# One block for the front and the heads of an mLSTM layer: context turned once and kept, gate scans in two halves, a division in two parts

## The reference

```python
ig, fg = concat(q, k, v) @ Wi + bi, concat(q, k, v) @ Wf + bf
log_f_cum = cumsum(log_sigmoid(fg))              # over the 256 positions
log_D = where(lower, log_f_cum[s] - log_f_cum[t], -inf) + ig[t]
max_log_D = max(log_D, -1)
D = exp(log_D - max_log_D)
C = (qh @ kh.T / sqrt(32)) * D
normalizer = maximum(abs(C.sum(-1)), exp(-max_log_D))
h = (C / (normalizer + 1e-6)) @ vh
hn = (h - mean(h)) * rsqrt(var(h) + 1e-6) * ln_scale   # per head
x = x + hn
```

## Time and profile before

| | us |
|---|---|
| median of 3 runs (1358.73 to 1361.98) | 1360.01 |
| the profiled execution, its own time | 1359.84 |
| its span | 1358.0 |
| PE, DVE busy | 1111.0, 845.8 |
| ACT, POOL busy | 515.9, 433.0 |

### The profile page before, as it was taken

One profiled execution on the slowest core, in us unless ns is written; L12 is line 12 of the kernel. 1 busy time (PEld: TensorE's weight loads), 2 busy tenths in 40 slices (PEclk: granted clock), 3 DMA queues, 4 the chain that ended last, 5 costly groups with the idle time before them and its releaser, 6 DMA issues. The chain is left out here.

```text
span 1358.0 us, 22418 instructions
## 1 busy us (share of the span) xinstructions
PE 1111.0 (82%) x6240; PEld 844.4 (62%) x6258; DVE 845.8 (62%) x1593; ACT 515.9 (38%) x1083; POOL 433.0 (32%) x336
## 2 busy tenths in 40 slices
PE   6999799789884827889835999499999999999942
PEld 6989666444442516878734876377777777777730
DVE  3434459678863616787836697656767677666415
ACT  2332152466661226666613315033333333333310
POOL 0000001111100100576782200155666656556520
PEclk9999799999997967787866999699999999999975
DMA  6220500000002748554107330477878888877539
GB/s 234 93 71 0 201 1 0 1 0 0 0 1 84 253 140 265 147 184 148 53 0 275 131 70 33 167 172 190 234 195 239 190 233 235 202 198 186 94 49 370
DMA packets 117836, 181.25 MB, mean 133 GB/s; under 512 B 13625, under 2 KB 48953, under 8 KB 117792
## 3 DMA queue, kind: packets, MB, share of 16 engines
q1 hardware_dynamic: 97408, 137.40, 31.4%
q0 software_dynamic: 18080, 38.85, 14.3%
q10 hardware_dynamic: 2304, 4.46, 0.9%
HBM read 138.76 MB, written 46.93 MB: 137 GB/s over the span
## 5 line engine op out<-in xcount | busy, mean ns | idle before, releaser
L2138 POOL DMA_INDIRECT y_d<-x_eo,x_ox x80 | 167.7, 2096 | 138.7 <-ACT x_eo L2291 108.1
L1486 POOL DMA_INDIRECT x_g<-r_d,x_ix x82 | 87.4, 1066 | 150.8 <-issue 118.4
L2195 PE MATMUL x_h<-x_w_hi,x_t_hi 128*128 x320 | 127.7, 399 | 2.2 <-DVE x_t_lo L2307 2.2
L2196 PE MATMUL x_h<-x_w_lo,x_t_hi 128*128 x320 | 127.3, 398 | 0.0
L2197 PE MATMUL x_h<-x_w_hi,x_t_lo 128*128 x320 | 127.2, 398 | 0.0
L204 POOL TENSOR_TENSOR ln_rstd<-ln_ve,powers 128x2 f32<-128x2 f32 (+1 forms) x40 | 25.6, 639 | 291.4 <-DVE ln_ve L198 291.4
L2307 DVE TENSOR_TENSOR x_w_lo<-w,x_w_hi (+1 forms) x64 | 109.5, 1752 | 0.1
L2267 ACT ACTIVATE x_gs<-x_h 128x256 f32<-128x256 f32 x80 | 30.7, 385 | 191.9 <-PE x_h L2197 163.3
L2307 DVE TENSOR_TENSOR x_t_lo<-x_xb,x_t_hi 128x512 fp32r<-128x512 f32 x80 | 55.2, 692 | 43.1 <-ACT x_t_hi L2262 38.1
L1412 DVE SCALAR_TENSOR_TENSOR h_c<-h_qk,h_d 128x768 f32<-128x768 f32 x64 | 58.1, 949 | 34.3 <-PE h_qk L1361 30.7
L1312 ACT ACTIVATE h_d<-h_negm,h_g 128x256 f32<-128x256 f32 x128 | 63.9, 499 | 37.4 <-DVE h_negm L1401 36.1
(11 more groups left out here) (351 smaller groups left out, 2729.8 us busy)
## 6 DMA issues: line engine op xcount, KB each, us to landing
w<-in_L_ffn_w SPq DMA_DIRECT2D x32, 1024.0 KB
h_negm<-negm_d SPq DMA_DIRECT2D x16, 1024.0 KB, 9.2
w<-in_L_ffn_w SPq DMA_DIRECT2D x32, 512.0 KB
raw<-in_L_ffn_w SPq DMA_DIRECT2D x3, 2816.0 KB, 16.6
x_res<-in_x SPq DMA_DIRECT2D x8, 512.0 KB, 4.7
ctx_in<-in_ctx SPq DMA_DIRECT2D x8, 512.0 KB, 4.0
m_cx<-in_ctx SPq DMA_DIRECT2D x8, 512.0 KB, 4.0
qt_d<-m_qt SPq DMA_DIRECT2D x8, 512.0 KB, 4.6
```

Of the source, the lines that this page charges most:

```text
L1486: nc.gpsimd.indirect_dma_start(out=xg[q][s][:], out_offset=None, in_=r_d, in_offset=bass.IndirectOffsetOnAxis(ap=ix[q][:, s:s + 1], axis=0 ...
L2138: nc.gpsimd.indirect_dma_start(out=y_d[s], out_offset=bass.IndirectOffsetOnAxis(ap=ox[q][:, s:s + 1], axis=0), in_=eo[q][s][:], in_offset= ...
L2195: nc.tensor.matmul(hbank[s][:], hi[:, k, :], w13p[0][:, at, k, :], start=k == 0, stop=False)
L2196: nc.tensor.matmul(hbank[s][:], hi[:, k, :], w13p[1][:, at, k, :], start=False, stop=False)
```

## The change

It has four parts.

1. The turned context is kept: `retention` stores `ct` per batch in DRAM (`kt_d`), from SP; DVE waits before the next copy into `ct` until the store has landed. The front no longer loads, turns or copies the context: it loads `kt_d` back, for the gates (two buffers `ak`) and later for the heads.
2. Weights, biases, ln_scale and the mask are loaded at the start of `bit_ffn` (`early`).
3. The three blocks of `mlstm` are one. The front has two sets of `Norm` tiles, and DVE takes the moments of batch b + 1 before it normalises b. PE turns b + 1 before the gates of b. Gate rows go from SBUF to SBUF. The gate scans are in two halves: half 0 (batches 0 to 3) right behind the front, half 1 inside the first batch of the heads. The loads of the first two batches of the heads that don't need `negm` are issued in the front.
4. `divide` keeps its first five instructions at k=0; the mean is now `mean`, at k=1 behind the mask.

```diff
@@ retention, SP
+            def keep_keys(b):
+                sp.wait_ge(ct_sb, 2 * b + 2)
+                sp.dma_start(kt_d[ds(b, 1)]..., ct[:]...).then_inc(kt_out, 16)
@@ retention, SP: in the loop behind the context load, and after it for the last two batches
+                    keep_keys(2 * i + u)
+            sp.wait_ge(kt_out, 16 * B + 16)
@@ retention, DVE
             def batch(b, nxt):
+                dve.wait_ge(kt_out, 16 * b + 16)
                 copies(b, ct_ps, None, (1, 3), lambda c: ct[:, :, c * P:(c + 1) * P], ct_sb)
@@ bit_ffn, SP (it had no program): loads of m_wraw, m_bias, ln_scale, future; then
+        sp.wait_ge(early_in, 96)
@@ mlstm, SP
+        keys(0)
+        keys(1)
+        for b in range(B - 1):
+            store_q(b)                      # waits xt_sb
+            if b + 2 < B:
+                sp.wait_ge(g_ps, b + 1)
+                keys(b + 2)                 # kt_d -> ak[b % 2], 512 KB
+            gate_rows(b)                    # waits g_sb; 2 DMAs into ig, fg
+            if b in (2, 3):
+                values(b - 2, b - 2)        # context rows of the heads
+                sp.wait_ge(q_stored[b - 2], 16)
+                scores(b - 2, b - 2)        # queries and keys of the heads
+        store_q(B - 1)
+        store_negm(0)
+        gate_rows(B - 1)
+        sp.wait_ge(negm_out, 16)
+        for u in range(2):
+            decays(u, u)                    # the negm rows, broadcast
+        ...
+        store_negm(1)
+        sp.wait_ge(negm_out, 32)
+        with sp.Fori(0, B // 2 - 1) as i:   # values, decays, scores of b + 2, as before
@@ mlstm, ACT
+        def soft_log(n):
+            r = part(n)                     # 64 of the 128 rows
+            act.wait_ge(rows_in[n], 2 * BB * 16)
+            steps.then(nc.scalar.activation(soft[r], fg[r], ACT.Abs))
+            steps.then(nc.scalar.activation(soft[r], soft[r], ACT.Exp, scale=-1.0))
+            nc.scalar.activation(soft[r], soft[r], ACT.Ln, bias=1.0).then_inc(soft_ready, 1)
+        queries(0)
+        for b in range(1, B):
+            queries(b)
+            if b == B - 2:
+                soft_log(0)
+            gates(b - 1)
+        gates(B - 1)
+        floors(0)
@@ mlstm, ACT, first batch of the heads
+                if first and k == 1: soft_log(1)
+                if first and k == 3: floors(1)
+            if first: act.wait_ge(t_sb, 4)
@@ mlstm, PE
+        turn(0)
+        for b in range(1, B):
+            turn(b)
+            gates(b - 1)                    # waits kt_in, xt_sb, g_sb of b - 3
+        gates(B - 1)
+        turn_back(0)
@@ mlstm, DVE
+        moments(0)
+        moments(1)
+        normalise(0)
+        for b in range(1, B):
+            if b + 1 < B:
+                moments(b + 1)
+            normalise(b)                    # waits xt_ps of b - 1, half by half
+        gate_scan(0)                        # six instructions on 64 rows
+        gate_columns(0)
@@ mlstm, DVE, in a batch of the heads
                 if k == 0 and not first:
                     divide(b - 1, 1 - u)
+                if k == 1 and not first:
+                    mean(b - 1, 1 - u)
                 if k == 3 and not first:
                     variance(b - 1)
+                if first and k == 2:
+                    gate_scan(1)
+            if first:
+                gate_columns(1)
+                dve.wait_ge(t_sb, 4)
```

More of the change, by code:

```diff
@@ L160, in program @@
             with ExitStack() as st:
-                mlstm(nc, st, sem, sbuf, psum, scratch_dram, a, x, ctx_rows, ident, powers, upto)
+                mlstm(nc, st, sem, sbuf, psum, scratch_dram, a, x, ctx_rows, ident, powers, early, kt_d, upto)
+        front.close()
         if upto >= 4:
@@ L354, in _ @@
             normalise(0, 0, 0)
+            dve.sem_inc(kt_out, 16)
             with steps.loop(0, B // 2 - 1, 8) as i:
@@ L637, in _, with bit_ffn @@
                 residual(B - 1, c)
-def bit_ffn(nc, st, sem, sbuf, psum, x, ident, powers, tern, w_mean):
+def bit_ffn(nc, st, sem, sbuf, psum, a, x, ident, powers, tern, w_mean, early):
     w1t = sbuf(st, "w1t", [P, KD, F0], BF16)
@@ new lines, in mlstm @@
+    xn = sbuf(st, "m_xn", [P, CB, D])
+    aq = sbuf(st, "m_qt", [P, 2, KD, S])
+    ak = sbuf(st, "m_kt", [P, 2, KD, S])
+    gts = sbuf(st, "m_gts", [2 * NH, B, S])
+    norms = [Norm(nc, st, sem, sbuf, f"ln2{u}", CB) for u in range(2)]
+    names = ("ig", "fg", "soft", "cum", "g", "m", "negm", "fl", "zero")
+    ig, fg, soft, cum, g, mx, negm, fl, zero = (sbuf(st, "d_" + n, [BH, S]) for n in names)
+    qt = sbuf(st, "h_qt", [P, 2, KD, S])
+    kt = sbuf(st, "h_kt", [P, 2, KD, S])
+    cx = sbuf(st, "h_cx", [P, 2, CB, D])
@@ new lines, in mlstm @@
+    qk = psum(st, "h_qk", [P, HG, 512])
+    pvb = [psum(st, f"h_pv{i}", [P, CB, HG + WIDE - 1, W]) for i in range(2)]
+    gbank = [t[:].rearrange("p c h w -> p (c h w)")[0:2 * NH, 0:S] for t in pvb]
+    tg = [psum(st, f"d_tg{j}", [P, CB, BH]) for j in range(2)]
+    w_sum, a_step, g_step, xn_ready, xt_ps, xt_sb, g_ps, g_sb = (
+        sem("m_" + n) for n in ("w_sum", "a_step", "g_step", "xn_ready", "xt_ps", "xt_sb", "g_ps", "g_sb"))
+    kt_in = [sem(f"m_kt_in{u}") for u in range(2)]
+    q_stored = [sem(f"m_q_stored{u}") for u in range(2)]
@@ new lines, in mlstm, with after, batches, part @@
+    block = st.enter_context(nc.Block())
+    LOADS = 5 * 16
+    OPEN = 2
+    HH = HG // 2
+    def after(eng, semaphore, value):
+        if not isinstance(value, int) or value > 0:
+            eng.wait_ge(semaphore, value)
+    def batches(eng, first, middle, last):
+        first(0, 0, 0)
+        with eng(0, B // 2 - 1) as i:
+            middle(2 * i + 1, i, 1)
+            middle(2 * i + 2, i + 1, 0)
+        last(B - 1, B // 2 - 1, 1)
+    def part(n):
+        return slice(BB * NH * n, BB * NH * (n + 1))
```

758 lines of the change are left out of this document (340 added, 418 removed).

## The result

The changed kernel takes 1311.47 us (median of 4 runs, 1309.77 to 1313.56) against 1359.37 for the kernel before on the same chip (1357.34 to 1361.98): a ratio of 0.9647 [0.963, 0.9664], 48 us less. The forecast was 1305.4 in a range of 1293 to 1327. The profiled execution took 1313.15 us, with a span of 1311.4 (before: 1359.84 and 1358.0).

The account below looks back on a forecast made before the run. Bound: rings through the engines in front and heads, where DVE's pile at k=0 cools PE, plus load waits. -5.5 - 10.0 - 19.7 + 2.5 - 19.2 - 2.5 = -54.4 from 1359.84 gives 1305.4 us; range 1293 to 1327.

Parts of the forecast that it names:

- The division and the clock: Heads, batches 1 to 6: moving the mean to k=1 shortens PE's pause and DVE's wait for scores; -19.2 us.
- The price of POOL beside DVE: Heads: DVE runs slower beside POOL, adding about 0.2 us to a batch of 19 us.
- The 3.2: Heads: gain per batch taken for the division in two, 19.2 us for six; bounds 0.3 and 3.9 a batch.
- The kept keys and the start: Storing kept keys in the retention costs 0; early loads bring the front's first transposes 5.5 us sooner.
- The gap: Last gates to first mask: half 0 scanned early, leaving issue and two broadcasts, 10.1 us; -19.7 us.
- The rounds of the front: First transposes to last gates: PE bounds rounds of 4.4 to 4.8 us, 43.1 us in all; -10 us.
- its 3.5 us for keys: Front: allowance for late key loads within the 43.1 us from first transposes to last gates.
- What is late next is the key load: Front: key loads are needed 5.3 us after issue; hidden at 4.0 us landing, 0.7 a round at 6.2.
- Batch 0: First batch of the heads: half 1's gates add about 2.5 us beyond 21.55; bounds 0 and 8.
- The tail: Batch 7 and tail: POOL's chain for batch 6 ends some 2.5 us earlier; -2.5 us (0 to -4).
- Slow keys and clock: Rival: the front waits for keys every round (+7) and the clock falls each batch (+7); 1320 us, chance 0.23.
- A PE at 1.2 GHz throughout: Rival, slower than before: small pauses keep PE at 1.2 GHz in heads and front; 1395 us, chance 0.03.

Follow-up runs that it names:

- the undivided: The changed kernel with the mean put back behind the division at k=0: 1327.51 us, ratio 0.9764 to the kernel before.
- the lengthened ones: The changed kernel with the division's product computed a second time, half of it (1318.89 us) or all of it (1336.16 us).

## Why the prediction was right, and where it was not

**The division and the clock** (-19.2, measured -19.9): right in place, cause and size. The step said that the pile between weigh(k=0) and weigh(k=1) cools PE and that DVE gets the cold back as its own wait. The changed kernel shows neither, the undivided and the lengthened ones both. The size is a little lucky: the six whole kernels with the same order in their heads and no work added took 113.4 to 115.5 us for these batches, as the clock fell in some of them once or twice. What the prediction left open, whether the shorter pause would do, was closer than it said: in the changed kernel 13 pauses up to 0.9 us left the clock at 1.00, in others some of 0.69 to 0.98 were followed by a fall, and in the two kernels with longer pauses, of 1.2 to 3.6 us, it fell in 11 batches of 12.

The price of POOL beside DVE was put too low, at 0.2 us a batch: in batches 1 to 6 the masks went from 34.4 to 36.6 us and the small instruction of the mean from 2.6 to 5.6, 0.9 a batch. The 3.2 had room for it.

**The kept keys and the start** (0 and -5.5, measured -0.9 and -6.0): right. The block begins 0.9 us earlier than before, so no delay by the eight stores is seen; among the kernels with this same part the first transposes come at 423.9 to 425.6, so the 0.9 is no gain either.

**The gap** (-19.7, measured -19.0): right. The broadcasts are issued at 473.69 and end 9.5 us later. One detail was off without a price: the prediction had `negm` in DRAM before gate_rows(7), but its store is issued at 471.06 and lands 2.6 us later, at 473.7, when the gate rows (issued from 472.48) are just out. The run with the half scan later shows that the overlap was needed for it.

**The rounds of the front** (-10.0, measured -5.0): here a step failed. Without its 3.5 us for keys the forecast was 39.6 us, and the kernel with the loads later, where PE waits for no keys, takes 40.5. So the bound and the round were right (4.6 us, inside the 4.4 to 4.8). The other 7.5 us of the changed kernel are:

- 1.0 at the cold start, ahead of any early load;
- 3.4 for keys, the 3.5 that was put down, though nearly all in one round behind the early loads, and nothing in the others;
- 1.5 for gate matmuls at a clock of 0.54 behind that pause (457.08 to 460.27), which the sum had at nothing;
- 1.6 behind that round, of which 1.4 is PE's wait for queries that ACT copies late.

The last item is the missed transfer. "What is late next is the key load" named only one of two that PE's new rhythm calls for. The other is the store of queries, behind which ACT waits 12.7 us, and which SP issues behind waits for gates and the 3 MB. The prediction followed SP's order for the keys and not for the queries. Setting that order right gave back 2.0 us, about the 1.4 and 0.75 of the pause for keys. So the missed store is the smaller part of the 5.0; the clock behind the pause, the start and the 0.9 by which 40.5 is above 39.6 are the rest. Issuing the loads later isn't a way to the forecast: the 6.5 us that they cost the front then come back as 6.9 in the gap.

**Batch 0** (+2.5, measured +3.1): right in size and cause. With the gates out it is 22.1 to 23.4 us in three kernels, with them in 23.4 to 24.7 in eight; in both sets it tends to be longer the later PE comes to its full clock. Between kernels where that is about 13 us behind the first mask (21.5 before, 23.9 with the loads later) and 14.4 us (22.1 and 24.6) the gates cost 2.4 us; where it is near 17 us (23.2 to 23.4 and 24.7), 1.3 to 1.5. The other 0.6 of the 3.1 is PE's later rise. By the Trainium skill ("ScalarE: Activation LUTs", What ACT_TABLE_LOAD costs) the first batch should have been about 2.7 us longer still. The trace doesn't agree: ACT's timeline in batch 0 of the changed kernel shows a load of 1.28 us with the next activation 0.02 us behind it:

```profile
494.23 1.28 ACT L1211 ACT_TABLE_LOAD   x1
495.53 0.41 ACT L1211 ACTIVATE d_soft<-d_soft 64x256 f32<-64x256 f32 x1
```

**The tail** (-2.5, measured -0.2): the term failed. POOL's chain for batch 6 did get shorter, by 3.5 us: it ends 26.7 us behind weigh(k=0) of batch 7 (647.88), for 30.2 before. But then POOL waits 3.23 us for batch 7's mean, which I hadn't followed. The mean is late by a fall of the clock, which slows the values of k=3, and with them later DVE's division comes to stand beside POOL's product and addition, where two of its instructions take 3.4 us more. PE's timeline in batch 7 of the changed kernel, and the stretches behind the pause:

```profile
632.91 0.71 PE L1327 MATMUL h_qk<-h_qt,h_kt 32*128 32x256 f32 x4 [1.00 <-DVE h_c L1419]
```

```profile
633.00:637.00 4.00, 4.00 (x25) 3.52 (x26) 3.49 (x4) 1.06 (x1) 2.77 (x3) 0.64 0.00 0
637.00:641.00 4.00, 4.00 (x21) 4.00 (x21) 0.73 (x2) 0.38 (x1) 3.89 (x2) 0.51 0.00 0
```

In the kernel with the early loads later, whose heads are the same, the pause at that place was 0.51 us and the clock held:

```profile
634.00:638.00 4.00, 4.00 (x38) 3.84 (x37) 3.71 (x4) 1.44 (x2) 2.68 (x3) 1.00 0.00 0
```

There the division's first instructions stand beside POOL's power and take their usual 0.2 us, only its last meets POOL's product, and the mean is ready 24.2 us behind the first weigh, ahead of POOL, for 29.9 in the changed kernel:

```profile
644.26 1.10 DVE L1438 TENSOR_SCALAR h_mu<-h_mu 128x32 f32<-128x32 f32 x1
```

Its tail took 42.3 us, 3.5 less than before the change: the forecast's size, where the clock allows it. (In this kernel the clock had fallen once in batch 6, behind a pause of 0.88 us at 613.82, and was full again at 620, before batch 7 began.) Before the change the mean was ready 27.7 us behind the first weigh, with POOL's chain at 30.2, so it held nobody; with POOL at 26.7 it is next. The Trainium skill ("GPSIMD Engine Reference", 8. Key points) has POOL and DVE share SBUF interfaces, with contention where DVE reads two inputs or is in a mode with two ports; the trace agrees that there is contention, and one of the instructions held is a TENSOR_SCALAR of one tensor (L1428, 2.25 us for 0.18). In which mode it ran no trace here shows.

The rivals: none of them came as a whole. Slow keys and clock had the direction of the front's miss: keys were late in one round and not in every one, and the clock fell behind that pause, but in batches 1 to 6 it didn't fall. A PE at 1.2 GHz throughout was seen in no run.

## What to carry to other kernels

When an engine's pile of work stalls PE, measure the pause beside the granted clock behind it: a microsecond of work put onto the pile cost 1.9 to 2.5 us (7.8 us for 4, 18.8 for 7.5), and one moved off it gave 1.3 to 1.5 (15.3 and 16.7 us for six times 1.9), because the clock moved with it. When a stage gets faster, list every transfer that a buffer waits for, stores as well as loads, and what is ahead of each in its queue; large loads moved early are not free, they only choose whom they delay. And when a chain is shortened, follow the other inputs of its next step before the gain is booked.

## What the runs showed of the hardware

- Some DVE instructions that begin while POOL's product or addition over [128 x 1024] runs end with it, within 0.06 us: [128 x 32] ones took 1.50 and 2.25 us for 0.2, and 1.10 for 0.18 in six of the batches. POOL's power over [128 x 32] held none of them, and a TENSOR_REDUCE from [128 x 1024] took its usual 1.21 us beside the addition (629.66). With the two POOL instructions made small a batch went from 18.9 to 17.9 us.
- Granted clock behind a pause of PE in the heads: up to 0.6 us it stayed 1.00 in every case looked at; 0.7 to 0.9 us, either, the same place in the program differing between kernels with equal heads (0.69 us: held at 514.16 in the changed kernel, fell at 511.35 with the queries first); 0.98 to 1.01 us, a fall each of eight times; 1.2 to 3.6 us, a fall in 11 of the 12 batches of the two kernels with longer pauses; the twelfth had a pause of 1.95 us.
- A store of 64 KB issued within 2.7 us behind four transfers of 512 KB landed 8.2 us after its issue, 2.6 us in the changed kernel; the changed front's stores of queries and loads of keys, 512 KB each, took a median of 3.7 us.
